# Rows 3 and 2 of the attention weights turned by VectorE and common transfers instead of by TensorE, with two rounds of buffers instead of three

## The chip, the cores and the metric

The kernel runs on one core of a Trainium2 chip. The metric is device time in microseconds; lower is better. Instructions run in order on each of five engines: TensorE (PE), VectorE (DVE), ScalarE (ACT), GpSimd (POOL) and SyncE (SP), which only starts transfers here. Engines wait for each other by semaphores.

## The reference

For x of 8 x 1024 tokens with 256 features the kernel computes `x + attention(layernorm(x)) + experts(layernorm(x))`, all in float32.

```python
qkv = jnp.einsum('bse,ehd->bshd', x, w_qkv)          # 16 heads of 64
logits = jnp.einsum('bqhd,bkhd->bhqk', q, k) / sqrt(64)
probs = softmax(where(causal_mask, logits, neg))
out = jnp.einsum('bshd,hde->bse', einsum('bhqk,bkhd->bqhd', probs, v), w_out)
```

The expert part routes each token to two of eight experts (256 to 1024 to 256, with relu), each with room for a limited number of tokens. The change touches the attention alone, which is also where the two parts are summed.

## The kernel before, in words

Layer norm, routing and the experts come first (about 900 us). Then `attention_and_sum` goes through 64 units, one for each batch and pair of heads. Precise products are made as three products of split operands (high and low parts), so each projection has a high copy by ScalarE and a low subtraction by VectorE.

A unit has the queries in eight rows of 128. Row i sees i + 1 blocks of 128 keys. The rows go in five rounds, `ROUNDS = [(3, 2), (4, 1), (5, 0), (6,), (7,)]`, each of four steps, so a unit has 20 steps. A round is a chain over the engines, for both heads h:

- TensorE: scores of the round into PSUM tile `S` (L1231). They wait until the minima of the round before are done, since `S` is used again.
- VectorE: row minima of the masked, negated scores, with a copy to SBUF, into a "room" `pr` (L1355).
- ScalarE: exponentials in place, with row sums (L1293).
- VectorE: reciprocals of the sums (L1361), at the start of the next round.
- GpSimd: scaling by the reciprocals, in place (L1436).
- Turning: the product with the values needs the weights with keys on the partitions.

There are two ways of turning. Rows 3, 2, 1 and 0 are transposed in 128x128 blocks by TensorE into a work bank in PSUM (L1187) and copied by ScalarE to `pT` (L1283). Rows 4 to 7 are transposed in squares of 32x32 by VectorE into `squares` (`square`, L1398), and transfers in strips of 32 partitions put them where they belong in `pT` (`place` on SyncE, L1085, and `place_rest` on GpSimd, L1465); there are 16 transfers for a group of two rows. Only after turning is a room free. `RING = 3` rounds of rooms take turns.

The product with the values (`values`, L1263) works on groups of two rows: one run for groups 0 and 1, one for group 2, one for group 3, each in the unit after. The result goes through ScalarE and VectorE (`oh`, `ol`) to the output projection (pieces o0 to o3, L1176), which VectorE adds to `res`.

Between the scores TensorE does pieces of other work in one of three PSUM banks: p0 to p3 (projections to q and k of the next unit, L1142), v0 and v1 (values of the pair after, L1157), xn (transposes of an input tile, L1165), t1 and t0 (rows 1 and 0 turned), o0 to o3. The order on all engines is written out by tables: `STEP_OF` says at which step TensorE does a piece, `ACT_STEP` and `DVE_STEP` at which step ScalarE and VectorE take it out of its bank, `BANK_OF` in which bank it lies, `RUN_STEP` when the values run, `POOL_AT` what GpSimd does when. Within a step VectorE does, in this order: reciprocals, the subtraction of a run, the pieces of the step, minima, and the squares of the round before in the third step of a round (`x == 2`). ScalarE does a run's copy, then pieces, then one exponential a step.

In the last unit all rows are turned by TensorE.

Of the kernel before, what the change touches and what calls it, by code (L numbers as in the profile page):

```python
# [16 lines left out]
P = 128  # L17
# [828 lines left out]
def attention_and_sum(nc, k, x, xn_dram, w_qkv, w_out, pick, y_dram, out, start):  # L846
# [10 lines left out]
    BL = 32  # L857
# [7 lines left out]
    SCALE_ORDER = [(i, h) for rows in ROUNDS for i in (rows if 0 not in rows else rows[::-1]) for h in range(2)]  # L865
# [10 lines left out]
    SQUARED = [4, 5, 6, 7]  # L876
    in_squares = lambda n, i: i in SQUARED and n < UNITS - 1


    TURNS = {"t30": [(3, 0, 0, 4)], "t31": [(3, 1, 0, 4)], "t20": [(2, 0, 0, 3)], "t21": [(2, 1, 0, 3)],  # L880
             "t1": [(1, 0, 0, 2), (1, 1, 0, 2)], "t0": [(0, 0, 0, 1), (0, 1, 0, 1)]}
    TURNS |= {f"t{i}{h}{c}": [(i, h, c * HT, min(HT, i + 1 - c * HT))] for i in SQUARED for c in range(-(-(i + 1) // HT)) for h in range(2)}


    STEP_OF = {"v0": 0, "xn": 1,
               "v1": 4, "o0": 5,
               "t30": 8, "t31": 8, "t20": 8, "t21": 8, "o1": 9, "p1": 10, "o2": 11,
               "p0": 12, "t1": 13,
               "t0": 16, "p2": 16, "p3": 17, "o3": 18}
# [17 lines left out]
    RUN_STEP = [(1, 3), (1, 7), (1, 15)]  # L907
# [11 lines left out]
    POOL_AT = {"split_w": 1, "total": 4, "place3": 5, "choose": 6, "fetch0": 8, "fetch1": 9, "weigh": 13, "add": 14, "place2": 16, "split_wv": 17}  # L919
# [24 lines left out]
    with ExitStack() as c:  # L944
# [45 lines left out]
        with ExitStack() as pre:  # L990
# [73 lines left out]
        def strip(g, a, b):  # L1064

            to, of = slice(b * BL, (b + 1) * BL), slice(a * BL, (a + 1) * BL)
            return wide[g][to, a].rearrange("p x r -> p (x r)"), sq[g][of, b].rearrange("p x k i -> p (x k i)")

        @block.sync
        def _(e):  # L1070
# [28 lines left out]
            for n in range(UNITS):  # L1099
# [18 lines left out]
                if n < UNITS - 1:  # L1118
                    place(n, 2)
# [12 lines left out]
        def _(e):  # L1132
# [103 lines left out]
            def values(n, j):  # L1236
                groups = RUN_GROUPS[j]
                if in_squares(n, 2 * groups[0]):
                    g = groups[0]
                    e.wait_ge(placed[g].sem, placed[g].at(n + 1, 0))  # L1240
                    e.wait_ge(pool_placed[g].sem, pool_placed[g].at(n + 1, 0))
                else:
                    for m, name in [(turn_unit(n, t), t) for g in groups for i in (2 * g, 2 * g + 1) for t in turns_of(i)]:
                        if by_act(name):
                            e.wait_ge(act.sem, act.at(m, name))
                        else:
                            e.wait_ge(dve.sem, dve.at(m, name))
# [91 lines left out]
        def _(e):  # L1339
            def row_min(n, j):  # L1340
# [69 lines left out]
            for n, s in ALL + END + [(UNITS + 1, s) for s in range(SUB)]:  # L1410
# [15 lines left out]
                if x == 2 and 0 <= m < UNITS and in_squares(m, ROUNDS[q][0]):  # L1426
                    for h in range(2):
                        square(m, ROUNDS[q][0], h)

        @block.gpsimd  # L1430
        def _(e):
# [28 lines left out]
            def place_rest(n, g):  # L1460
                e.wait_ge(squared.sem, squared.at(n, 4 * g - 4))
# [109 lines left out]
```

## Time and profile before

| | us |
|---|---|
| median of 3 runs | 2915.57 (2914.02 to 2918.3) |
| the profiled execution | 2915.7, its span 2913.9 |
| TensorE busy | 2814.5, 97% of the span |
| VectorE busy | 2084.7, 72% |
| GpSimd busy | 1723.0, 59% |
| ScalarE busy | 1699.7, 58% |
| mean granted clock of TensorE | 0.988 |

The shares are means over all stages. The attention part is the second half of the page's slices and more: there TensorE shows 9 tenths in every slice, VectorE 8, GpSimd 7 or 8, ScalarE 6. A matmul's row shows its start and modelled end; rows overlap, so from start to start is what one costs. The chain that ended last lies on TensorE for 66% of the span, by the page.

### The profile page before, as it was taken

How to read it: one execution, taken by the hardware profiler on the slowest of the kernel's cores; microseconds unless marked ns; L12 is line 12 of the kernel's file. 1: busy time of each engine (PE TensorE's matmuls, PEld its weight loads, DVE VectorE, ACT ScalarE, POOL GpSimd, SP SyncE). 2: the span in 40 equal slices, each digit the busy share in tenths (PEclk: the TensorE clock that was granted, in tenths of full speed). 3: DMA queues.
4: the chain of work that ended last, by engine and by line, in shares of the span. 5: the costliest groups of instructions: out<-in, count | busy, mean ns of one | idle time of the engine just before them, and what ended most of it. 6: DMA issues, size and time to landing. Idle time of an engine off the chain costs nothing.

```text
span 2913.9 us, 61264 instructions
## 1 busy us (share of the span) xinstructions
PE 2814.5 (97%) x21321; PEld 2284.1 (78%) x21321; DVE 2084.7 (72%) x4448; ACT 1699.7 (58%) x3934; POOL 1723.0 (59%) x2631
## 2 busy tenths in 40 slices
PE   5599999999998999999999999999999999999998
PEld 4489999899997777777777777777777777777776
DVE  7843444344434888888888888888888888888886
ACT  3454444445454666666666666666666666666664
POOL 3032122211212777777877877777777778777774
PEclk9799999999999999999999999999999999999999
DMA  7022212221212565665665565665665556556553
GB/s 241 29 82 75 69 52 83 76 68 47 82 54 74 141 158 144 163 154 145 168 150 145 147 170 147 157 166 142 157 164 151 149 146 176 141 145 183 136 134 93
DMA packets 248774, 371.58 MB, mean 128 GB/s; under 512 B 77392, under 2 KB 177744, under 8 KB 248480
## 3 DMA queue, kind: packets, MB, share of 16 engines
q1 hardware_dynamic: 216000, 276.31, 35.3%
q0 software_dynamic: 32480, 91.44, 11.7%
q8 instruction: 174, 2.85, 0.4%
q14 instruction: 120, 0.98, 0.1%
HBM read 102.80 MB, written 33.55 MB: 47 GB/s over the span
## 4 chain that ended last, share of the span: by engine, by line
PE 66%; DVE 1%; SPq 1%; DMA 0%; issue 0%; ACT 0%; POOL 0%; DVEq 0%; ACTq 0%
PE O L1263 18%; PE S L1231 16%; PE W L1142 12%; PE W L1157 7%; PE W L1176 7%; PE W L1187 6%; SPq L1085 1%; DVE pr L1355 0%; PE W L1165 0%; DMA pT<-squares 0%; DVE squares L1398 0%; ACT pr L1293 0%; DMA out<-res 0%; ACT pT L1283 0%; DVE res L1381 0%
## 5 line engine op out<-in xcount | busy, mean ns | idle before, releaser
L1436 POOL TENSOR_SCALAR pr<-pr,rinv 128x512 f32<-128x512 f32 (+7 forms) x1024 | 748.4, 744 | 399.7 <-DVE rinv L1361 398.6
L1293 ACT ACTIVATE pr<-pr,negm 128x512 f32<-128x512 f32 (+7 forms) x1024 | 787.3, 774 | 285.3 <-DVE negm L1355 285.3
L1355 DVE CUSTOM_DVE_ANT_0 pr<-S,late 128x512 f32<-128x512 f32 (+7 forms) x1024 | 717.0, 751 | 112.9 <-PE S L1231 112.9
L1263 PE MATMUL O<-pT,vv 128*64 128x256 f32 (+1 forms) x5120 | 541.3, 362 | 3.1 <-DMA pT<-squares 3.1
L1398 DVE STREAM_TRANSPOSE squares<-pr 128x640 f32<-128x640 f32 x504 | 494.8, 1020 | 0.0
L1263 PEld LDWEIGHTS O<-pT,vv 128*64 128x64 f32 x5120 | 346.4, 137 | 181.8 <-issue 20.4
L832 DVE TENSOR_TENSOR hl<-h,hh 128x512 fp32r<-128x512 f32 x256 | 192.3, 751 | 315.2 <-ACT hh L793 315.0
L789 ACT ACTIVATE h<-pH,b1c 128x512 f32<-128x512 f32 x256 | 175.9, 687 | 366.0 <-PE pH L719 334.1
L1283 ACT ACTIVATE pT<-W 128x512 f32<-128x512 f32 (+3 forms) x520 | 199.6, 437 | 215.8 <-PE W L1187 215.8
L731 PE MATMUL pY<-w2h,hh 128*128 128x256 f32 x1024 | 287.7, 281 | 2.5 <-DVE hl L832 2.5
L731 PE MATMUL pY<-w2l,hh 128*128 128x256 f32 x1024 | 289.1, 282 | 0.0
L731 PE MATMUL pY<-w2h,hl 128*128 128x256 f32 x1024 | 288.0, 281 | 0.0
L1465 POOL DMA_DIRECT2D pT<-squares x504 | 258.8, 521 | 0.3 <-issue 0.2
L1231 PE MATMUL S<-khf,qh 64*128 64x512 f32 (+2 forms) x1024 | 218.6, 422 | 3.6 <-DVE negm L1355 3.6
L1142 PE MATMUL W<-xnh,wh 128*128 128x512 f32 x512 | 215.1, 420 | 3.0 <-DVE klf L1389 1.5
L719 PE MATMUL pH<-xh,w1h 128*128 128x512 f32 x512 | 205.5, 401 | 4.2 <-DVE xl L804 2.6
L664 POOL COPY idx<-slot_token 128x4 uint32 (+1 forms) x30 | 8.8, 293 | 335.3 <-PE pX L705 335.3
L1142 PE MATMUL W<-xnl,wh 128*128 128x512 f32 x512 | 203.2, 397 | 0.0
L1142 PE MATMUL W<-xnh,wl 128*128 128x512 f32 x512 | 203.1, 397 | 0.0
L719 PE MATMUL pH<-xh,w1l 128*128 128x512 f32 x512 | 201.5, 394 | 0.0
L719 PE MATMUL pH<-xl,w1h 128*128 128x512 f32 x512 | 201.4, 393 | 0.0
L1381 DVE TENSOR_TENSOR res<-W,res 128x512 f32<-128x512 f32 x256 | 175.6, 686 | 35.6 <-PE W L1176 25.4
(176 smaller groups left out, 6479.6 us busy)
## 6 DMA issues: line engine op xcount, KB each, us to landing
pT<-squares SPq DMA_DIRECT2D x756, 128.0 KB
pT<-squares SPq DMA_DIRECT2D x756, 96.0 KB, 2.8
pT<-squares POOLq DMA_DIRECT2D x252, 128.0 KB
pT<-squares POOLq DMA_DIRECT2D x252, 96.0 KB, 3.0
y<-yb SPq DMA_DIRECT2D x128, 128.0 KB, 1.7
wr<-in_L_attn_w_qkv SPq DMA_DIRECT2D x128, 128.0 KB, 2.3
x<-in_L_attn_x SPq DMA_DIRECT2D x16, 512.0 KB, 8.9
xn<-xn SPq DMA_DIRECT2D x16, 512.0 KB, 4.4
```

What stands on the lines that cost most here:

```text
L719: ins = e.matmul(pH[hc % 4][:], w[par][:, m, ws], xx[q][:, m, :], start=(n == 0), stop=(n == 3 * MC - 1))
L731: ins = e.matmul(pY[t % 2][:], hs[q][:, hc, ts_], ws[par][:, hc, :], start=(hc == 0 and n == 0), stop=(hc == HC - 1 and n == 2))
L1142: ins = e.matmul(W, ws[:, 2 * m + of_k], xs[:, t0:t0 + HT, m, :], start=(i == 0), stop=(i == 3 * MC - 1))
L1157: ins = e.matmul(W[:, t * VW:(t + 1) * VW], xs[:, t0 + t, m, :], ws[:, m, :], start=(j == 0), stop=(j == len(terms) - 1))
L1176: ins = e.matmul(W[:, t * MODEL:(t + 1) * MODEL], os_[:, ts_], ws[:, of % PAIRS, :], start=(i == 0), stop=(i == 2))
L1231: ins = e.matmul(S[h][:, off + f * HALF:off + f * HALF + cols], t[hs, i * P:(i + 1) * P], u[f][n % 2][hs, 0:cols], start=(j == 0), stop=(j ...
L1263: ins = e.matmul(O[hs, o0 + a:o0 + GQ], vv[n // 2 % 2][:, kt, vs], turned_p, start=(kt == 0), stop=(kt == KT - 1))
L1293: e.activation(p, p, ACT.Exp, bias=negm[:, c0:c0 + 1], scale=-1.0, accum_out=rsum[:, c0:c0 + 1]).then_inc(expd.sem, 1)
L1355: e.tensor_tensor_reduce(room_of(n, i, h)[:, off:off + w], S[h][:, off:off + w], late[:, SEQ - w:], 1.0, -MASKED, ALU.add, ALU.min, negm[: ...
L1398: e.transpose(sq[g][:, :, 2 * h + i % 2, 0:KT, :], room_of(n, i, h)[:, OFFSET[i]:OFFSET[i] + KT * P].rearrange("p (k b i) -> p b k i", b=Q ...
L1436: e.tensor_scalar(p, p, rinv[:, c0:c0 + 1], 1.0, ALU.mult, ALU.mult).then_inc(scaled.sem, 1)
L1465: e.dma_start(*strip(g, QUARTERS - 1, b)).then_inc(pool_placed[g].sem, 16)
```

## The change

VectorE turns rows 3 and 2 (group 1) like rows 4 to 7: four more squares a unit, behind the minima of round 1. Groups 1 and 2 share tiles (`pT12`, `squares12`), so that one strip holds both: 16 transfers of 160 KB in place of 16 of 96 KB, all started by SyncE once row 5 is done; GpSimd starts 4 for group 3 alone. Fourteen transposes of TensorE and four copies of ScalarE go away. The larger squares take the space of a round of rooms: `RING` is 2. Row 1's transposes (t1) move from step 13 to 8, row 0's (t0) from 16 to 12, and both are scaled first in their rounds. The first run of values moves from step 3 to 7, and the tables are set anew. In the last unit only rows 6 and 7 are turned by TensorE.

```diff
-    SUB, RING = 4, 3
+    SUB, RING = 4, 2
-    SCALE_ORDER = [... (rows if 0 not in rows else rows[::-1]) ...]
+    SCALE_ORDER = [... (rows if 3 in rows else rows[::-1]) ...]
-    SQUARED = [4, 5, 6, 7]
-    in_squares = lambda n, i: i in SQUARED and n < UNITS - 1
+    SQUARED = [(i, h) for i in (3, 2, 4, 5, 6, 7) for h in range(2)]
+    in_squares = lambda n, i: i > 1 and (n < UNITS - 1 or i not in TURNED_LAST)
...
-    DVE_STEP = {"xn": 3, "o0": 6, "o1": 10, "p1": 12, "o2": 12, "p0": 15, "p2": 19, "p3": 19, "o3": STEPS + 2}
+    DVE_STEP = {"xn": 2, "p1": 6, "o0": 10, "o1": 10, "p0": 14, "o2": 15, "p2": 18, "p3": 19, "o3": STEPS}
...
-    RUN_STEP = [(1, 3), (1, 7), (1, 15)]
+    RUN_STEP = [(1, 7), (1, 11), (1, 15)]
...
+        pT12, sq12 = (sb(n, [P, QUARTERS, BLOCK[1] + BLOCK[2]]) for n in ("pT12", "squares12"))
...
             def place(n, g):
-                e.wait_ge(squared.sem, squared.at(n, 4 * g - 4))
+                e.wait_ge(squared.sem, squared.at(n, 4 * g))
...
-                for a in range(QUARTERS - 1):
+                for a in range(QUARTERS - (g == 3)):
...
             def square(n, i, h):
-                if n > 0 and i % 2 == 0 and h == 0:
-                    e.wait_ge(placed[g].sem, placed[g].at(n, 0))
-                    e.wait_ge(pool_placed[g].sem, pool_placed[g].at(n, 0))
+                if n > 0 and i in (3, 6) and h == 0:
+                    e.wait_ge(placed[max(g, 2)].sem, placed[max(g, 2)].at(n, 0))
...
-                if x == 2 and 0 <= m < UNITS and in_squares(m, ROUNDS[q][0]):
-                    for h in range(2):
-                        square(m, ROUNDS[q][0], h)
+                if x == 2 and 0 <= m < UNITS:
+                    for i in ROUNDS[q]:
+                        if in_squares(m, i):
+                            for h in range(2):
+                                square(m, i, h)
```

What the tables do to the order is seen in three places of a steady unit. On VectorE, between the minima of round 0 and of round 1 (`xnl` is piece xn, `squares 128x4x256` are row 7 of the unit before, `res` is an output piece, `ol` a run's subtraction), there stood before:

```order
L1381 TENSOR_TENSOR res<-W,res 128x512
L1398 STREAM_TRANSPOSE squares<-pr 128x4x256 x2
L1371 TENSOR_TENSOR xnl<-W,xnh 128x256
L1361 RECIPROCAL rinv<-rsum 128x4
L1405 TENSOR_TENSOR ol<-O,oh 128x512
L1355 ISA pr,negm<-S,late 128x640
```
and there stands now:

```order
L1379 TENSOR_TENSOR xnl<-W,xnh 128x256
L1407 STREAM_TRANSPOSE squares<-pr 128x4x256 x2
L1369 RECIPROCAL rinv<-rsum 128x4
L1363 ISA pr,negm<-S,late 128x640
L1363 ISA negm 128x1
```
The piece xn is ahead of the squares instead of behind them; the output piece and the run's subtraction are gone from here.

On VectorE, from the last minimum of round 1 to the first of round 2 (`klf` is piece p1), before:

```order
L1355 ISA pr,negm<-S,late 128x256
L1355 ISA negm 128x1
L1381 TENSOR_TENSOR res<-W,res 128x512
L1361 RECIPROCAL rinv<-rsum 128x4
L1405 TENSOR_TENSOR ol<-O,oh 128x256
L1355 ISA pr,negm<-S,late 128x768
```
and now:

```order
L1363 ISA pr,negm<-S,late 128x256
L1363 ISA negm 128x1
L1397 TENSOR_TENSOR klf<-W,khf 128x512
L1407 STREAM_TRANSPOSE squares<-pr 128x4x128 x2
L1407 STREAM_TRANSPOSE squares<-pr 128x4x96 x2
L1369 RECIPROCAL rinv<-rsum 128x4
L1414 TENSOR_TENSOR ol<-O,oh 128x512
L1363 ISA pr,negm<-S,late 128x768
```
Piece p1 and the four new squares stand ahead of the reciprocals of round 1.

On TensorE, behind the scores of round 2 (`W<-ident,pr` are transposes: fourteen of rows 3 and 2 before, four of row 1 now; `W<-woh,oh` and the like are an output piece), before:

```order
L1231 MATMUL S<-khf,ql 128x256 x2
L1187 MATMUL W<-ident,pr 128x128 x14
L1176 MATMUL W<-woh,oh 128x256
L1176 MATMUL W<-wol,oh 128x256
L1176 MATMUL W<-woh,ol 128x256
L1176 MATMUL W<-woh,oh 128x256
L1176 MATMUL W<-wol,oh 128x256
L1176 MATMUL W<-woh,ol 128x256
L1142 MATMUL W<-xnh,wh 128x512
```
and now:

```order
L1238 MATMUL S<-khf,ql 128x256 x2
L1194 MATMUL W<-ident,pr 128x128 x4
L1183 MATMUL W<-woh,oh 128x256
L1183 MATMUL W<-wol,oh 128x256
L1183 MATMUL W<-woh,ol 128x256
L1183 MATMUL W<-woh,oh 128x256
L1183 MATMUL W<-wol,oh 128x256
L1183 MATMUL W<-woh,ol 128x256
L1183 MATMUL W<-woh,oh 128x256
```
The transposes that stand here are now of a row of the round just ahead, and two output pieces follow them.

## Rows read from the trace of the kernel before

**Rows 1.** Window: length; busy PE, PEld, DVE, ACT, POOL; granted clock; DMA share; GB/s.
```profile
2000.00:2500.00 500.00, 500.00 (x4005) 388.52 (x4002) 419.81 (x930) 321.20 (x812) 388.14 (x617) 1.00 0.59 154
```

**Rows 2.** Timeline of VectorE, one unit: start, length (us), engine, line, operation.
```profile
2001.25 0.67 DVE L1355 CUSTOM_DVE_ANT_0 pr<-S,late 128x512 f32<-128x512 f32 x1
...
2003.41 0.69 DVE L1381 TENSOR_TENSOR res<-W,res 128x512 f32<-128x512 f32 x1
2004.01 2.36 DVE L1398 STREAM_TRANSPOSE squares<-pr 128x1024 f32<-128x1024 f32 x2
2006.30 0.38 DVE L1371 TENSOR_TENSOR xnl<-W,xnh 128x256 fp32r<-128x256 f32 x1
2006.61 0.16 DVE L1361 RECIPROCAL rinv<-rsum 128x4 f32<-128x4 f32 x1
...
2007.26 0.81 DVE L1355 CUSTOM_DVE_ANT_0 pr<-S,late 128x640 f32<-128x640 f32 x1
...
2009.43 0.69 DVE L1381 TENSOR_TENSOR res<-W,res 128x512 f32<-128x512 f32 x1
...
2016.44 1.56 DVE L1398 STREAM_TRANSPOSE squares<-pr 128x640 f32<-128x640 f32 x2
...
2018.63 0.69 DVE L1389 TENSOR_TENSOR klf<-W,khf 128x512 fp32r<-128x512 f32 x1 [0.31 <-ACT khf L1313]
...
2026.50 1.23 DVE L1355 CUSTOM_DVE_ANT_0 pr<-S,late 128x1024 f32<-128x1024 f32 x1 [0.87 <-PE S L1231]
...
2028.80 2.10 DVE L1398 STREAM_TRANSPOSE squares<-pr 128x896 f32<-128x896 f32 x2
...
2032.06 0.67 DVE L1355 CUSTOM_DVE_ANT_0 pr<-S,late 128x512 f32<-128x512 f32 x1
```

**Rows 3.** Timeline of TensorE, the same unit.
```profile
2008.85 2.60 PE L1263 MATMUL O<-pT,vv 128*64 128x256 f32 x24
2011.38 0.50 PE L1231 MATMUL S<-khf,qh 64*128 64x512 f32 x2
...
2012.98 1.89 PE L1187 MATMUL W<-ident,pr 128*128 128x128 f32 x14
...
2017.02 0.28 PE L1176 MATMUL W<-woh,oh 128*128 128x256 f32 x1
...
2017.83 0.50 PE L1231 MATMUL S<-khf,qh 64*128 64x512 f32 x2
...
2019.25 0.50 PE L1142 MATMUL W<-xnh,wh 128*128 128x512 f32 x1
...
2020.76 0.60 PE L1187 MATMUL W<-ident,pr 128*128 128x128 f32 x4
2021.29 3.46 PE L1263 MATMUL O<-pT,vv 128*64 128x256 f32 x32
...
2026.27 0.44 PE L1187 MATMUL W<-ident,pr 128*128 128x128 f32 x2
```

**Rows 4.** Timeline of ScalarE, the same unit.
```profile
2003.86 0.37 ACT L1299 ACTIVATE xnh<-W 128x256 fp32r<-128x256 f32 x1
...
2009.76 0.57 ACT L1304 ACTIVATE vv<-W 128x512 f32<-128x512 f32 x1
...
2017.99 0.60 ACT L1313 ACTIVATE khf<-W 128x512 fp32r<-128x512 f32 x1
...
2028.92 0.58 ACT L1313 ACTIVATE qh<-W 128x512 fp32r<-128x512 f32 x1
```

**Rows 5.** Timeline of GpSimd, the same unit.
```profile
2006.87 2.49 POOL L1436 TENSOR_SCALAR pr<-pr,rinv 128x512 f32<-128x512 f32 x4 [0.46 <-DVE rinv L1361]
```

**Rows 6.** Groups by form, scalings 256 wide: count, busy us, mean ns.
```profile
L1436 POOL TENSOR_SCALAR pr<-pr,rinv 128x256 f32<-128x256 f32 x32 | 14.8, 469 | 0.0
```

**Rows 7.** SyncE's transfers by line: ns of one issue, least, median, most.
```profile
L1085 SPq DMA_DIRECT2D pT<-squares x385: 507/592/1642, 1999.8 to 2492.9; - x193
```

**Rows 8.** Windows, ten microseconds near the start; columns as in rows 1.
```profile
30.00:40.00 10.00, 6.74 (x73) 5.38 (x66) 9.69 (x42) 4.30 (x14) 2.68 (x2) 0.73 1.04 366
```

More of the change, by code:

```diff
@@ L861, in attention_and_sum @@
     ROUNDS = [(3, 2), (4, 1), (5, 0), (6,), (7,)]
-    SUB, RING = 4, 3
+    SUB, RING = 4, 2
     STEPS = SUB * len(ROUNDS)
     ORDER = [(i, h) for rows in ROUNDS for i in rows for h in range(2)]
-    SCALE_ORDER = [(i, h) for rows in ROUNDS for i in (rows if 0 not in rows else rows[::-1]) for h in range(2)]
+    SCALE_ORDER = [(i, h) for rows in ROUNDS for i in (rows if 3 in rows else rows[::-1]) for h in range(2)]
     PLACE = {row: j for j, row in enumerate(ORDER)}
@@ new lines, in attention_and_sum @@
+    TURNS = {"t1": [(1, 0, 0, 2), (1, 1, 0, 2)], "t0": [(0, 0, 0, 1), (0, 1, 0, 1)]}
+    TURNS |= {f"t{i}{h}{c}": [(i, h, c * HT, min(HT, i + 1 - c * HT))] for i in TURNED_LAST for c in range(-(-(i + 1) // HT)) for h in range(2)}
+    STEP_OF = {"v0": 0, "xn": 1, "v1": 2,
+               "p1": 4,
+               "t1": 8, "o0": 9, "o1": 10,
+               "t0": 12, "p0": 12, "o2": 13,
+               "p2": 16, "p3": 17, "o3": 18}
+    ACT_STEP = {"v0": 2, "xn": 2, "v1": 4, "p1": 6, "t1": 8, "t0": 12, "p0": 13, "p2": 17, "p3": 18}
@@ L899, in attention_and_sum @@
+    DVE_STEP = {"xn": 2, "p1": 6, "o0": 10, "o1": 10, "p0": 14, "o2": 15, "p2": 18, "p3": 19, "o3": STEPS}
+    BANK_OF = {"v0": 0, "xn": 2, "v1": 1,
+               "p1": 2,
+               "t1": 2, "o0": 1, "o1": 0,
+               "t0": 2, "p0": 1, "o2": 0,
+               "p2": 0, "p3": 1, "o3": 2}
+    END_STEP = {6: (UNITS, 0), 7: (UNITS, 4)}
     DVE_STEP |= {f"t6{h}{c}": 2 for h in range(2) for c in range(2)}
@@ L953, in attention_and_sum @@
         vv = two(lambda i: sb(f"vv{i}", [P, QT, VW]))
-        pT = [sb(f"pT{g}", [P, 2, 2 * g + 2, GQ]) for g in range(GROUPS)]
-        sq = {g: sb(f"squares{g}", [P, QUARTERS, 4, 2 * g + 2, BL]) for g in (2, 3)}
-        wide = {g: pT[g][:].rearrange("p h k q -> p (h k q)").rearrange("p (a x r) -> p a x r", x=4, a=QUARTERS) for g in (2, 3)}
+        BLOCK = {g: 4 * (2 * g + 2) * BL for g in (1, 2, 3)}
+        pT0, pT3 = (sb(f"pT{g}", [P, 2, 2 * g + 2, GQ]) for g in (0, 3))
+        pT12, sq12 = (sb(n, [P, QUARTERS, BLOCK[1] + BLOCK[2]]) for n in ("pT12", "squares12"))
+        sq3 = sb("squares3", [P, QUARTERS, BLOCK[3]])
+        pT = {0: pT0[:], 3: pT3[:]}
+        wide = {1: pT12[:, :, :BLOCK[1]], 2: pT12[:, :, BLOCK[1]:],
+                3: pT3[:].rearrange("p h k q -> p (h k q)").rearrange("p (a r) -> p a r", a=QUARTERS)}
+        wide = {g: w.rearrange("p a (x r) -> p a x r", x=4) for g, w in wide.items()}
+        sq = {1: sq12[:, :, :BLOCK[1]], 2: sq12[:, :, BLOCK[1]:], 3: sq3[:]}
+        sq = {g: w.rearrange("p b (x k i) -> p b x k i", x=4, i=BL) for g, w in sq.items()}
+        whole = {2: (pT12[:], sq12[:]), 3: (wide[3].rearrange("p a x r -> p a (x r)"), sq3[:])}
         pr = start.pr + [sb(f"pr{i}", [P, SEQ]) for i in range(len(start.pr), 2 * RING)]
@@ L1026, in _ @@
             def _(e):
-                for g in (2, 3):
+                for g in (1, 2, 3):
                     e.memset(sq[g][:, :, 0::2, 2 * g + 1, :], 0.0)
@@ L1066, in strip @@
             to, of = slice(b * BL, (b + 1) * BL), slice(a * BL, (a + 1) * BL)
-            return wide[g][to, a].rearrange("p x r -> p (x r)"), sq[g][of, b].rearrange("p x k i -> p (x k i)")
+            placed_in, squares = whole[g]
+            return placed_in[to, a], squares[of, b]
         @block.sync
@@ L1117, in _ @@
                         refill(b, g)
-                if n < UNITS - 1:
-                    place(n, 2)
+                place(n, 2)
                 if n % 2 == 0 and n // 2 + 2 < UNITS // 2:
@@ L1237, in values @@
                 groups = RUN_GROUPS[j]
[L1238 to L1247, printed above, removed]
+                for g in groups:
+                    if in_squares(n, 2 * g):
+                        e.wait_ge(placed[max(g, 2)].sem, placed[max(g, 2)].at(n + 1, 0))
+                        if g == 3:
+                            e.wait_ge(pool_placed.sem, pool_placed.at(n + 1, 0))
+                    else:
+                        for m, name in [(turn_unit(n, t), t) for i in (2 * g, 2 * g + 1) for t in turns_of(i)]:
+                            if by_act(name):
+                                e.wait_ge(act.sem, act.at(m, name))
+                            else:
+                                e.wait_ge(dve.sem, dve.at(m, name))
                 if j == 0:
@@ L1518, in _ @@
                         place_rest(n - 1, 3)
-                    elif name == "place2" and n < UNITS - 1:
-                        place_rest(n, 2)
                     elif name == "choose":
```

33 lines of the change are left out of this document (10 added, 23 removed).

## The prediction

> **What bounds the kernel now.** I read the windows first, then one steady unit engine by engine. In 500 us of the attention part TensorE is busy for all 500.00 us, VectorE for 419.81, GpSimd for 388.14 and ScalarE for 321.20, and the granted clock is 1.00 [rows 1]. The reader should look for a gap in TensorE's list of a unit and find none: every row starts before the one ahead of it has ended [rows 3]. VectorE waits only where it needs scores, for 0.87 us before the minima of round 4 [rows 2]. So before the change TensorE sets the length of a unit: from the minima of round 0 to those of the next unit 2032.06 - 2001.25 = 30.81 us [rows 2], and there are 64 units.
>
> I write M0 to M4 for the moments at which VectorE starts the minima of rounds 0 to 4. In before M0 to M1 is 6.01 us and M4 to the next M0 is 5.56 [rows 2].
>
> **Part 1: fourteen transposes leave TensorE.** They take 1.89 us [rows 3]; nothing of rows 3 and 2 remains there. If TensorE stayed without gaps, a unit would take 30.81 - 1.89 = 28.92 us. The three copies of 512 columns and one of 384 that brought them from PSUM to SBUF leave ScalarE, which has slack [rows 1] and gains nothing I count.
>
> **Part 2: four transposes come to VectorE.** The trace has no pair 512 or 384 wide. A pair 1024 wide takes 2.36 us, one 640 wide 1.56 [rows 2]: 0.267 us for each 128 columns, which gives 1.29 and 1.03, less 0.07 each that the next instruction overlaps (2.36 long, but 2.29 from start to start): 2.18 us. Bounds: not above two pairs 640 wide, 3.12; not below what four copies of a plain 256-wide operation would cost at 0.31 (2006.30 to 2006.61 [rows 2]), 1.24. I take 2.18, since the shape of the instruction is the same and only the width differs. VectorE's work is then 419.81/500 x 30.81 + 2.18 = 25.87 + 2.18 = 28.05 us a unit, 97% of 28.92. Its waits decide.
>
> The Trainium skill, "VectorE: DVE Perf Modes", section Rules for kernel authors, speaks against the move: a full 128x128 transpose belongs on TensorE where PSUM will do as its target, and VectorE only turns 32x32 blocks. The rows agree mildly: TensorE pays 1.89/14 = 0.135 us a block, VectorE 2.18/14 = 0.156, and the blocks still need transfers. By the rule the trade loses 0.29 us of engine time a unit, by the trace it also moves the work to the engine that is about to be the fuller one.
>
> **Part 3: new places in VectorE's order make three waits.** In each, VectorE now takes a piece ahead of the squares that it took behind them, and the piece needs a ScalarE copy that stands behind two exponentials. (a) The subtraction of xn: the copy starts at 2003.86 and lasts 0.37 [rows 4], and 0.04 pass before VectorE can start (copy of khf 2017.99 + 0.60, subtraction 2018.63 [rows 4, 2]). So it starts at M0 + 3.02, while the minima end at M0 + 2.16 (2003.41): 0.86 of waiting. (b) p1: two exponentials of round 1 end at 2009.76, M1 + 2.50 [rows 4]; then the copy (0.60 + 0.04): M1 + 3.14 against minima that end at M1 + 2.17 (2009.43): 0.97. (c) p2: its copy starts at 2028.92 [rows 4], M4 + 2.42; with 0.58 and the same 0.04 VectorE can go on at M4 + 3.04, while the minima end at M4 + 2.30 (2028.80): 0.74. In before the squares (2.29 us after the minima of round 0, 2004.01 to 2006.30) covered exactly these copies. p0 gets such a wait too, but in round 3, where VectorE has room (below).
>
> **Part 4: row 1's four transposes now stand one round earlier.** In before, row 1 was turned on TensorE in round 3; now right behind the scores of round 2. Row 1 must first be scaled by GpSimd, that needs the reciprocals of round 1, and these stand on VectorE behind p1 and all four new squares. TensorE goes in order, so everything behind t1 waits: o0, o1, the values of group 2, the scores of round 3.
>
> **The sum, once round the unit.**
> M0 to M1: xn starts at 3.02, takes 0.31, squares of row 7 2.29, reciprocals 0.05 (0.65 from them to the next minima, with a 512-wide subtraction of 0.60 between, [rows 2]): 5.67.
> M1 to the reciprocals of round 1: 3.14, p1 0.60 (as 2003.41 to 2004.01), new squares 2.18: 5.92.
> Reciprocals to t1: 0.26 (2006.61 [rows 2] to 2006.87 [rows 5]), two scalings 256 wide at 0.47 [rows 6], 0.15 for GpSimd to TensorE (my choice between 0.04 above and the 0.23 from TensorE to VectorE, 2026.27 to 2026.50): 1.35.
> t1 to M3: t1 0.53 (2020.76 to 2021.29), two output projections at 0.81 (2017.02 to 2017.83), values of group 2 2.53 (2008.85 to 2011.38), scores of round 3 1.42 (2017.83 to 2019.25), 0.23: 6.33 [rows 3].
> M3 to M4 is TensorE's: 7.02 in before (2019.25 to 2026.27), without t1 0.53, with t0 0.27 and o2 0.81: 7.57.
> M4 to the next M0: 5.56 + 0.74 of (c) + o3, which now stands here, 0.60: 6.90.
> Together 33.74 us, against 30.81: +2.93.
>
> Is each leg the later of the two engines? TensorE reaches t1 early: scores of round 1 once the minima of round 0 are done (M0 + 2.16), 1.60, p1 1.51, values of groups 0 and 1 not over 2.53, scores of round 2 1.60 (2011.38 to 2012.98 [rows 3]): M0 + 9.40, while t1 can start at 5.67 + 5.92 + 1.35 = M0 + 12.94. It stands still for some 3.5 us. VectorE reaches the minima of round 3 early: 0.60 + 2.17 + 1.20 + 1.56 + 0.05 = 5.58 after the reciprocals, against 1.35 + 6.33. At M4 TensorE needs 1.51 + 1.51 + 0.81 + at most 1.60 = 5.43 to the end of the next scores, less than 6.90.
>
> **What I cost at nothing.** Two rounds of rooms instead of three: a room's squares already stand ahead of the minima that refill it, on the same engine. The common transfers: squares of row 5 are done by about M3 + 5.2; 16 issues at 0.592 [rows 7] take 9.5, so the last leaves at M3 + 14.7, and the squares of row 3 of the next unit, the first to need it landed, come at M3 + 7.57 + 6.90 + 5.67 + 3.74 = 23.9. That leaves 9 us for a landing; each further us would be one us a unit. The group read in strips by the values of group 1: hidden in TensorE's 3.5 us.
>
> 63 steps from unit to unit x 2.93 = 185 us. The profiled execution took 2915.7 us (span 2913.9, 1.8 around it), the median is 2915.57: the same. 2915.7 + 185 = 3100 us, my forecast. With the bounds of part 2 (-0.94 to +0.94 a unit) this case runs from 3041 to 3160.
>
> **Rivals.** (A) TensorE stays the bound: 28.92 a unit, 2915.7 - 63 x 1.89 = 2797 us. For it: TensorE had no gap at all. Against it: VectorE would have to be 97% busy with none of its three waits. (B) Only t1's wait is hidden, because VectorE runs ahead of my chain; then VectorE alone sets 28.05 + 0.86 + 0.97 + 0.74 = 30.62, -0.19 a unit: 2904 us, no change that could be told. Against it: the reciprocals stand behind the squares in the same queue, so nothing lets them run ahead. (C) Slower still: TensorE's clock falls after its new 3.5 us of standing. In 30 to 40 us of this trace TensorE was busy for 6.74 us of ten and the granted clock 0.73 [rows 8]: between full speed (2.4 GHz) and half of it, 54% of these ten us at half, which costs 2.7 us of work. Once a unit and wholly on the leg from t1 to M4 that is 33.74 + 2.7: 2915.7 + 63 x 5.63 = 3270 us; it decides from the point where the clock in a steady window drops below about 0.95. The Trainium skill, "TensorE: Matmul & The Clock Gate", section Why this matters for your kernels, warns of idle gaps between bursts for this reason; by it C would be the likeliest. The steady stretch shows 1.00 with no gap to test it on, and the new gap is a tenth of a unit where the slow stretch stood idle for a third.
>
> **Chances.** The forecast 0.68, C 0.14, B 0.10, A 0.08. Faster or slower means by over 0.2%, about 6 us; less than that cannot be told from no change here. Faster: A and half of B, 0.13; same: the other half, 0.05; slower: 0.82. The range leaves out A, B and the far end of C: 2990 to 3240; its low end is there for waits that overlap more than I let them.
>
> **What would show it.** Right: a unit near 33.7 us, TensorE's transposes of row 1 waiting some 3.5 us for GpSimd's scaling, VectorE waiting for ScalarE's copies at xn, p1 and p2, TensorE near 86% busy. Wrong: TensorE without a gap (A), a gap at t1 gone while VectorE is over 95% busy (B), a granted clock well below 1 (C), or VectorE's squares of row 3 waiting for transfers, which I priced at nothing.

## The result: slower by 7.4%, and the profile after

The changed kernel takes 3130.19 us (median of 4 runs, 3124.16 to 3133.84) where the kernel before takes 2914.8 on the same chip: a ratio of 1.0736, 95% interval 1.0713 to 1.0759. The forecast was 3100, the range 2990 to 3240. The profiled execution has a span of 3132.0 us, 218 more than before.

The page's busy times of the changed kernel, and then windows of it with the columns of [rows 1]: the same 500 us, one unit, and the unit ahead of it.

```profile
PE 2767.1 (88%) x20403; PEld 2237.2 (71%) x20403; DVE 2220.2 (71%) x4704; ACT 1589.3 (51%) x3674; POOL 1603.4 (51%) x2380
```

```profile
2000.00:2500.00 500.00, 439.24 (x3370) 338.15 (x3367) 403.42 (x876) 260.88 (x661) 314.77 (x485) 0.97 0.71 167
2017.82:2051.20 33.38, 29.27 (x232) 22.49 (x232) 27.83 (x62) 18.09 (x46) 23.14 (x37) 1.00 0.73 182
1982.94:2017.82 34.88, 30.74 (x232) 23.95 (x232) 28.00 (x62) 18.09 (x46) 20.96 (x33) 0.95 0.70 163
```

TensorE, without a gap in [rows 1], now stands for 12% of the time, and no other engine has become full: VectorE is busy for 403 of 500 us, less than before. So the time went into waits in a circle of engines, not into work. Two lengths of a unit stand side by side: 33.38 us at a granted clock of 1.00, and 34.88 at 0.95.

VectorE in the unit at clock 1.00, against [rows 2]: start, length, engine, line, operation, and in brackets the idle time before it and who ended it.

```profile
2017.82 0.67 DVE L1363 CUSTOM_DVE_ANT_0 pr<-S,late 128x512 f32<-128x512 f32 x1
...
2020.85 0.42 DVE L1379 TENSOR_TENSOR xnl<-W,xnh 128x256 fp32r<-128x256 f32 x1 [0.78 <-ACT xnh L1307]
2021.19 2.36 DVE L1407 STREAM_TRANSPOSE squares<-pr 128x1024 f32<-128x1024 f32 x2
...
2023.53 0.79 DVE L1363 CUSTOM_DVE_ANT_0 pr<-S,late 128x640 f32<-128x640 f32 x1
...
2026.62 0.69 DVE L1397 TENSOR_TENSOR klf<-W,khf 128x512 fp32r<-128x512 f32 x1 [0.85 <-ACT khf L1321]
2027.22 2.21 DVE L1407 STREAM_TRANSPOSE squares<-pr 128x512 f32<-128x512 f32 x4
2029.36 0.13 DVE L1369 RECIPROCAL rinv<-rsum 128x4 f32<-128x4 f32 x1
...
2036.87 1.09 DVE L1363 CUSTOM_DVE_ANT_0 pr<-S,late 128x896 f32<-128x896 f32 x1 [0.71 <-PE S L1238]
...
2044.32 1.23 DVE L1363 CUSTOM_DVE_ANT_0 pr<-S,late 128x1024 f32<-128x1024 f32 x1 [0.87 <-PE S L1238]
...
2047.35 0.69 DVE L1397 TENSOR_TENSOR ql<-W,qh 128x512 fp32r<-128x512 f32 x1 [0.65 <-ACT qh L1321]
...
2051.20 0.68 DVE L1363 CUSTOM_DVE_ANT_0 pr<-S,late 128x512 f32<-128x512 f32 x1
```

TensorE and GpSimd of the same unit, against [rows 3] and [rows 5]; of TensorE, the last piece ahead of its long wait is p1.

```profile
2020.22 0.50 PE L1238 MATMUL S<-khf,qh 64*128 64x512 f32 x2 [0.42 <-DVE negm L1363]
...
2022.53 0.47 PE L1149 MATMUL W<-xnh,wh 128*128 128x512 f32 x1 [0.64 <-ACT vv L1312]
...
2030.69 0.63 PE L1194 MATMUL W<-ident,pr 128*128 128x128 f32 x4 [2.60 <-POOL pr L1447]
```

```profile
2020.95 1.44 POOL L1459 TENSOR_TENSOR wl<-wr,wh 128x256 fp32r<-128x256 f32 x2
...
2026.17 0.73 POOL L1511 TENSOR_TENSOR res<-res,yg 128x256 f32<-128x256 f32 x1
2026.84 2.09 POOL L1476 DMA_DIRECT2D pT<-squares  x4
...
2029.60 2.50 POOL L1447 TENSOR_SCALAR pr<-pr,rinv 128x256 f32<-128x256 f32 x4 [0.47 <-DVE rinv L1369]
```

The reader should follow one hand-over: reciprocals of round 1 on VectorE at 2029.36, behind the four new squares; GpSimd's scaling of row 1 at 2029.60; TensorE's t1 at 2030.69, after 2.60 us of standing.

The length of all 63 intervals between the minima of round 0, before and after, accounts for the difference:

| intervals | before, us each | after, us each | difference, us |
|---|---|---|---|
| 47 plain ones, as if all at 33.40 | 30.81 | 33.40 | 121.6 |
| 28 of these, longer at the lower clock | | 34.86 | 40.8 |
| 7 in which a batch's output is stored | 30.6 to 32.7 | 35.5 to 39.1 | 39.0 |
| 7 plain ones at the end, without xn | 30.57 | 32.21 | 11.4 |
| the first two | 24.90, 34.02 | 30.94, 34.00 | 6.0 |

Together 218.8. The first and fourth lines are the chain of the forecast, the second is a falling clock. The third holds the chain too, and beyond it waits for transfers behind SyncE's queue and a clock of 0.95 or less in all seven; these two aren't separated here. The first two units are not traced back.

The clock, in windows of two microseconds of the longer unit:

```profile
1992.00:1994.00 2.00, 1.23 (x18) 0.93 (x14) 2.00 (x4) 1.17 (x5) 2.00 (x5) 1.00 0.86 213
1994.00:1996.00 2.00, 0.18 (x1) 0.21 (x2) 2.00 (x7) 0.00 (x0) 1.53 (x5) 0.92 0.98 281
1996.00:1998.00 2.00, 2.00 (x11) 2.00 (x11) 1.38 (x8) 1.06 (x3) 1.85 (x3) 0.50 1.05 250
1998.00:2000.00 2.00, 2.00 (x14) 1.65 (x15) 1.29 (x2) 2.00 (x7) 1.43 (x2) 0.72 1.02 227
2000.00:2002.00 2.00, 2.00 (x22) 1.32 (x20) 1.63 (x4) 0.25 (x3) 0.27 (x1) 1.00 0.31 84
```

TensorE stood 2.59 us ahead of t1, which starts at 1995.82. At about the end of that stand the granted clock fell to 0.50, the lower level of 1.2 GHz, and it was back at 2.4 in the window from 2000. The output projection's matmuls start 0.21 us apart at the lower level, and 0.12 in the other unit.

SyncE and then TensorE where a batch ends (the interval from 2051.20 is 36.5 us long):

```profile
2044.88 0.37 SPq L1102 DMA_DIRECT2D res<-in_L_attn_x  x1
2045.34 11.85 SPq L1093 DMA_DIRECT2D pT<-squares  x16
2057.24 1.74 SPq L1085 DMA_DIRECT2D wvr<-in_L_attn_w_qkv  x2
2059.02 0.51 SPq L1097 DMA_DIRECT2D out<-res  x1
2062.28 0.37 SPq L1102 DMA_DIRECT2D res<-in_L_attn_x  x1
```

```profile
2061.04 3.80 PE L1271 MATMUL O<-pT,vv 128*64 128x256 f32 x24 [3.47 <-issue]
```

The sixteen common transfers leave only behind the third quarter's store and refill, up to 2057.19. The first run of values of the next unit reads them and starts at 2061.04, after 3.47 us for which the row names no releaser. The last of the sixteen was issued at 2056.4 and took 4.4 us to land, so it landed at 2060.8, just ahead of the run; I read the wait as one for this landing, and experiment 6 tests it.

### The profile page after: what moved, and what is told of

Read it like the earlier page. It is cut to its first block and busy times, and to the rows that moved or that the text cites. A ratio compares the mean times of both kernels' runs of the same rounds, so it can differ in the third digit from the quotient of the medians.

```text
span 3132.0 us, 58788 instructions
## 1 busy us (share of the span) xinstructions
PE 2767.1 (88%) x20403; PEld 2237.2 (71%) x20403; DVE 2220.2 (71%) x4704; ACT 1589.3 (51%) x3674; POOL 1603.4 (51%) x2380
## 5 line engine op out<-in xcount | busy, mean ns | idle before, releaser
L1407 DVE STREAM_TRANSPOSE squares<-pr 128x512 f32<-128x512 f32 x764 | 639.4, 882 | 1.2 <-DMA pT<-squares 1.2
L1271 PE MATMUL O<-pT,vv 128*64 128x256 f32 (+1 forms) x5120 | 556.3, 369 | 31.9 <-issue 11.9
L1271 PEld LDWEIGHTS O<-pT,vv 128*64 128x64 f32 x5120 | 356.7, 140 | 227.6 <-issue 46.6
L1149 PE MATMUL W<-xnh,wh 128*128 128x512 f32 x512 | 219.7, 429 | 42.0 <-ACT vv L1312 34.4
L1291 ACT ACTIVATE pT<-W 128x256 f32<-128x256 f32 (+1 forms) x260 | 73.0, 332 | 304.7 <-PE W L1194 298.8
L1332 ACT ACTIVATE oh<-O 128x256 fp32r<-128x256 f32 (+1 forms) x192 | 86.5, 451 | 250.9 <-PE O L1271 250.7
L1194 PE MATMUL W<-ident,pr 128*128 128x128 f32 x414 | 85.3, 327 | 143.3 <-POOL pr L1447 139.8
L731 PEld LDWEIGHTS pY<-w2h,hh 128*128 128x128 f32 x1024 | 193.0, 188 | 7.9 <-issue 2.9
```

The source lines that it names most:

```text
L731: ins = e.matmul(pY[t % 2][:], hs[q][:, hc, ts_], ws[par][:, hc, :], start=(hc == 0 and n == 0), stop=(hc == HC - 1 and n == 2))
L1149: ins = e.matmul(W, ws[:, 2 * m + of_k], xs[:, t0:t0 + HT, m, :], start=(i == 0), stop=(i == 3 * MC - 1))
L1271: ins = e.matmul(O[hs, o0 + a:o0 + GQ], vv[n // 2 % 2][:, kt, vs], turned_p, start=(kt == 0), stop=(kt == KT - 1))
L1332: e.activation(oh[:, cols], O[:, cols], ACT.Copy).then_inc(ohi.sem, 1)
L1407: e.transpose(sq[g][:, :, 2 * h + i % 2, 0:KT, :], room_of(n, i, h)[:, OFFSET[i]:OFFSET[i] + KT * P].rearrange("p (k b i) -> p b k i", b=Q ...
```

## The experiments

Times are medians; the kernel before stood between 2914 and 2918 us beside them. BEH, NOPOOL and ORD name edits that later kernels use again.

**1. Filling TensorE's gap.** Nine matmuls of 512 columns, whose result nothing reads, ahead of t1.

```diff
+ if n < UNITS and s == 8:
+     e.wait_ge(act.sem, act.at(n if n + 1 < UNITS else n - 1, "v0"))
+     for j in range(9):
+         e.matmul(banks[0], wh[:, 0], xnh[:, 0:HT, 0, :], start=True, stop=True)
```

> The changed kernel with nine extra matmuls of 512 columns (some 2.1 us, their result is thrown away) on TensorE between the scores of round 2 and row 1's transposes, where it stands idle for 2.6 us. Theory (chain, and the clock falls because of that idle stretch): row 1's transposes start when they did, the chain is as long as before (33.4 us a unit), but no unit is seen at a granted clock of 0.95 any more, which 36 of 63 are in the changed kernel at 1.5 us each: about 3076 us, mean clock near 0.99. Rival 1 (the clock has another cause, the alternation of units is one of even and odd pairs): still 34.9 every other unit, about 3130. Rival 2 (TensorE is the bound after all): 63 x 2.1 us more, 3260.

3108.5 us, ratio 1.0656 (1.0636 to 1.0676). Windows of a unit, then the filler in it:

```profile
1967.61:2001.01 33.40, 31.59 (x241) 24.11 (x241) 27.84 (x62) 18.09 (x46) 20.97 (x33) 1.00 0.73 170
```

```profile
1977.82 2.37 PE L1283 MATMUL W<-xnh,wh 128*128 128x512 f32 x9
1980.49 0.63 PE L1194 MATMUL W<-ident,pr 128*128 128x128 f32 x4 [0.30 <-POOL pr L1451]
```

All plain units are 33.40 at clock 1.00: the standing time brought the clock down there, and the chain does not care whether TensorE works or waits. The clock still falls in four of the seven batch ends. These grew (36 to 39.5 us), and the last units to 32.9, so the total fell by 22 us and not by the 54 expected.

**2. The three pieces behind the squares again (BEH).**

```diff
- DVE_STEP = {"xn": 2, "p1": 6, ... "p2": 18,
+ DVE_STEP = {"xn": 3, "p1": 7, ... "p2": 19,
```

> The changed kernel with the pieces xn, p1 and p2 taken by VectorE behind the squares instead of ahead of them (DVE_STEP 3, 7 and 19 instead of 2, 6 and 18). Theory: the three waits for ScalarE's copies (0.78, 0.85 and 0.65 us in the changed kernel, 2.3 to 2.6 us with what hangs on them) leave the closed chain: 33.4 - 2.5 = 30.9 us a unit; TensorE's wait at row 1's transposes shrinks from 2.6 to about 0.6 us and the clock stays up: about 2930 us in all. Rival 1 (VectorE's own load and the transposes in it set the length): the load is the same, so the time moves by less than 0.5 us a unit, over 3080 us. Rival 2 (common transfers late): no change either.

2992.73 us, 1.0276 (1.0249 to 1.0303): the largest step of any experiment, 137 us. By the traces the shorter chain of the 47 plain units gives 100 us and the clock, which no longer falls in them, 41; the rest moved a little the other way. The plain unit falls by 2.13, to 31.27, though TensorE still waits:

```profile
1918.75 0.63 PE L1194 MATMUL W<-ident,pr 128*128 128x128 f32 x4 [0.98 <-POOL pr L1447]
```

In that unit the three legs with the moved pieces are shorter by 0.87, 0.96 and 0.73 us, 2.56 together as expected. The leg from the reciprocals to M3 gave 0.43 back (7.94 for 7.51): GpSimd starts the scaling 0.69 us after the reciprocals and not 0.24. The time missed the 2930 expected by 63 us, mostly at the batch ends, which are 36.6 to 38.9 us.

**3. t1 behind the output projections.**

```diff
- "t1": 8, "o0": 9, "o1": 10,
+ "o0": 9, "o1": 10, "t1": 11,
```
(and ScalarE's copy of it at step 12.)

> The changed kernel with row 1's transposes on TensorE moved from step 8 to 11, behind two output pieces (o0, o1). Theory: the pieces wait only for the subtraction of the first run, which VectorE does 0.6 us after the reciprocals of round 1, so TensorE goes on 0.8 us after them instead of 1.3: 0.5 us a unit less at the same clock (32.9), about 3095 us if the clock falls as often as now, down to 3045 if it stays up. Rival 1 (GpSimd's scaling of row 1 alone is what holds TensorE): taking it off the path wins far more, 2 us a unit or more, under 3000 us. Rival 2 (not this place holds the unit): no change.

3127.96 us, 1.0717 (1.0691 to 1.0743). The unit at clock 1.00 is 32.98, as expected, but 38 of the 47 plain units are 34.5 at 0.95, where 28 were at 0.95 in the changed kernel. The circle runs through o0 as well: it needs the first run's subtraction, which stands behind the same squares.

```profile
2029.81 0.53 PE L1183 MATMUL W<-woh,oh 128*128 128x256 f32 x1 [2.13 <-DVE ol L1414]
```

**4. The new squares one block wide.** Rows 3 and 2 are turned for 128 columns only; the rest of their transposing is left out.

```diff
+ KT = 1 if i < 4 else KT
```

> The changed kernel with VectorE's four squares of rows 3 and 2 cut to one block of 128 columns each (32 columns a strip), which leaves that part of the transposing out; transfers, waits and order are as before. Theory: the four squares take about 0.6 us instead of 2.15 and the reciprocals behind them come 1.5 us earlier: 31.9 us a unit and, with 1.1 us of idle time left at row 1's transposes, a clock that stays up: about 2985 us. Rival 1 (a chain that does not hold these squares sets the length): no more than 0.5 us a unit, over 3080 us.

3119.72 us, 1.0695 (1.0676 to 1.0715); 32.87 at clock 1.00, where 31.9 was expected, and 36 of the 47 plain units are some 34.4 at 0.95, where the clock was to stay up. The squares took 0.88 us, not 2.21, but GpSimd wasn't ready:

```profile
1954.84 0.88 DVE L1408 STREAM_TRANSPOSE squares<-pr 128x128 f32<-128x128 f32 x4
1955.64 0.14 DVE L1369 RECIPROCAL rinv<-rsum 128x4 f32<-128x4 f32 x1
```

```profile
1953.78 0.73 POOL L1512 TENSOR_TENSOR res<-res,yg 128x256 f32<-128x256 f32 x1
1954.45 2.08 POOL L1477 DMA_DIRECT2D pT<-squares  x4
1956.53 0.20 POOL L1482 COPY sel<-pick 128x4 uint32<-128x4 uint32 x1
1956.70 2.48 POOL L1448 TENSOR_SCALAR pr<-pr,rinv 128x256 f32<-128x256 f32 x4
```

The reciprocals came at 1955.64, the scaling 1.06 us later, behind four DMA issues. In the changed kernel GpSimd idled only 0.47 us there: whoever takes more than half a microsecond from the squares meets its queue. By the length of the unit alone, shorter by 0.53 us, the rival is nearly met (no more than 0.5); GpSimd's rows are why I read it otherwise, and the next experiment tests that.

**5. GpSimd issues none of the third group (BEH and NOPOOL).**

```diff
- for a in range(QUARTERS - (g == 3)):
+ for a in range(QUARTERS):
```
(and `place_rest` goes, with its semaphore.)

> e2_behind with the four transfers of group 3 that GpSimd starts (2.08 us of its time) started by SyncE with the other twelve. Theory (GpSimd's queue, full until half a microsecond after the reciprocals of round 1, is what held row 1's transposes in e4_small and e2_behind): TensorE's wait there shrinks from 0.98 to about 0.4 us, a steady unit from 31.27 to about 30.7 us, some 35 us in all, 2955 us; the units at a batch's end stay at 37 to 39 us or grow, since SyncE has four more transfers ahead of the common ones. Rival (VectorE's squares alone hold it): no change, 2990 us.

3003.0 us, 1.0306 (1.0285 to 1.0327), no better than experiment 2. The best units are 30.85, near the 30.7 expected, with TensorE's wait at t1 down from 0.98 to 0.56 us, so GpSimd's queue did hold it in part. But units scatter up to 32.4 and batch ends reach 37 to 40.5: SyncE now issues 32 strips a unit, and TensorE waits for the third group's.

**6. The common transfers ahead of the third quarter's store (BEH and this).**

```diff
-                    for g in range(3):
+                    for g in range(2):
                         store(b - 1, g)
-                    for g in range(3):
+                    for g in range(2):
                         refill(b, g)
                 place(n, 2)
+                if b > 0 and u == 0:
+                    store(b - 1, 2)
+                    refill(b, 2)
```

> e2_behind with SyncE's order changed in the first unit of a batch: the common transfers of groups 1 and 2 ahead of the store and refill of the third quarter of the output, instead of behind them. Theory: the seven units of 36.6 to 38.9 us against 31.3 are units in which the common transfers leave late, because SyncE waits for that store to land; with the new order they come down to 31 to 32.5 us, 40 us less in all: about 2950 us, steady units unchanged. Rival (the store's and refill's traffic slows them): no change, 2990 us.

3006.39 us, 1.0312 (1.0291 to 1.0334). It failed: batch ends are 40.0 to 40.8 us. The first run's wait is gone, but SyncE now stands for two landings of stores ahead of the third group, and another run of values waits:

```profile
1985.52 0.67 SPq L1097 DMA_DIRECT2D out<-res  x1
1990.13 0.37 SPq L1102 DMA_DIRECT2D res<-in_L_attn_x  x1
...
1992.13 18.21 SPq L1093 DMA_DIRECT2D pT<-squares  x27
```

```profile
2001.86 5.87 PE L1274 MATMUL O<-pT,vv 128*64 128x256 f32 x32 [6.30 <-DMA pT<-squares]
```

**7. All of these together.** BEH, NOPOOL, the order of experiment 6, t1 at step 11, p1 in another PSUM bank, p0 behind its squares too, and GpSimd's weight split one unit ahead.

```diff
-               "p1": 2,
-               "t1": 2, "o0": 1, "o1": 0,
+               "p1": 0,
+               "o0": 1, "o1": 0, "t1": 2,
...
-    POOL_AT = {"split_w": 1, ...
+    POOL_AT = {"split_w": 18, ...
```

> All together: pieces behind the squares (p0 too), all transfers by SyncE, the store order of e6_store, row 1's transposes behind o0 and o1, piece p1 in a bank that does not wait for xn, and GpSimd's split of the next weights at step 18 of the unit before instead of step 1. Theory: the waits of TensorE in e2_behind (0.18, 0.88 and 0.98 us a unit) go but for 0.3 us, so a unit is TensorE's 28.9 plus 0.3 to 0.8 us, and the whole takes 2810 to 2845 us, faster than both kernels. Rival (VectorE, 28.05 us of work and waits of its own of over 2 us, sets the length): over 30.1 us a unit, 2890 us or more.

2966.93 us, 1.0178 (1.0159 to 1.0198). The plain units are 30.44 to 31.15, 18 of 47 at 30.45 or less and most below the 30.81 of before, but none at the 29.2 to 29.7 expected. Six of the batch ends are 38.8 to 42.4. One long wait was left on TensorE in a unit:

```profile
1874.07 0.35 PE L1185 MATMUL W<-woh,oh 128*128 128x256 f32 x1 [1.02 <-DVE ol L1412]
```

**8. Fewer waits for a landing in SyncE's way (BEH and ORD).** Transfers go ahead of the later stores, and the refills of the last two quarters one unit later; the refills of the first two still wait for their stores.

```diff
                 if b > 0 and u == 0:
-                    for g in range(3):
+                    for g in range(2):
                         store(b - 1, g)
-                    for g in range(3):
+                    for g in range(2):
+                        refill(b, g)
+                if b > 0 and u == 1:
+                    for g in (2, 3):
                         refill(b, g)
                 place(n, 2)
+                if b > 0 and u == 0:
+                    store(b - 1, 2)
...
                     store(b - 1, 3)
-                    refill(b, 3)
```

> As e2_behind, with SyncE's order changed in the two units in which a batch ends: each common transfer is issued ahead of the store that waits for the later output projections, and the refills of the third and fourth quarter of the residual go one unit later, behind the third group's transfers, when their stores have long landed; nothing is left out. Theory (the long units at the ends of batches come from transfers that stand in SyncE's queue behind waits for stores): the 7 long units of e2_behind (36.6 to 38.9 us) come to 31.3 to 32 us, the others stay at 31.27, so 2993 - 7 x 6.2 = about 2950 us. Rival (the long units come from the bytes that stores, refills and strips move at the same time): they stay at 36 us or more and the time within 10 us of 2993.

2973.86 us, 1.0191 (1.0174 to 1.0208): 19 us better than experiment 2, where 43 were expected. The batch ends were 36.6 to 38.9 us and are now 33.5 to 37.1; what the seven take beyond plain units fell from 46 to 31 us together, by the traces, so the order of the queue was a third of it. In the unit from 1967.66, with the DMA engines at 0.95, TensorE still waited for the third group's strips:

```profile
1991.89 4.97 PE L1275 MATMUL O<-pT,vv 128*64 128x256 f32 x32 [4.24 <-DMA pT<-squares]
```

**9. ORD in the kernel of experiment 7, and p1 behind the first run's subtraction.**

```diff
- DVE_STEP = {"xn": 3, "p1": 7, ...
+ DVE_STEP = {"xn": 3, "p1": 8, ...
```

> As e7_all with the order of SyncE's queue of e8_order in place of its own, and with the subtraction of the key projection behind that of the first run of values on VectorE; nothing is left out. Theory: the boundary units of e7_all (38.8 to 42.4 us) fall to 30.5 to 31.5 (-62 us in all), and TensorE's wait of 1.02 us ahead of the first output projection falls to about 0.4, which takes a unit from 30.45 to about 29.9 (-30 us): 2967 - 62 - 30 = about 2875 us, under the kernel before. Rival (the unit is bound elsewhere on VectorE by then, and the order of two subtractions doesn't matter): units stay at 30.4 and the time is about 2905 us, no gain over the kernel before worth the name.

2910.54 us, 0.9981 (0.9970 to 0.9991): level with the kernel before. Batch ends 32.6 to 34.4, plain units 30.37 and not 29.9. The wait ahead of o0 fell from 1.02 to 0.64 only:

```profile
2030.12 0.36 PE L1186 MATMUL W<-woh,oh 128*128 128x256 f32 x1 [0.64 <-DVE ol L1413]
```

**10. GpSimd issues the refills.**

```diff
- POOL_AT = { ... "total": 4, ...
+ POOL_AT = { ... "total": 4, "fill2": 6, "fill3": 9, "fill0": 17, "fill1": 17, ...
```

> As e9_all, with all refills of the residual issued by GpSimd in place of SyncE; nothing is left out. In e9_all's unit 33 (33.01 us beside 30.37 for the others) SyncE issues without a pause from 1900 to 1958 us, each half of 16 strips in about 11.5 us, and TensorE waits 2.46 us for the third group's strips. Theory (SyncE's queue is too full in that pair of units: waits for stores and refills take 6 us of it): the 7 boundary units fall from 32.6 to 34.2 to 30.4 to 31, and the time by about 16 us, to 2895. Rival (the DMA engines, busy 0.93 of that unit, are full, and whoever issues doesn't matter): the units stay at 32.6 or more, the time at 2910.

2930.01 us, 1.0038 (1.0025 to 1.0051). My theory fell, and the time is above the rival's 2910 too: batch ends rose to 34.7 to 36.6, and TensorE's wait for the third group there is 3.99 us (2.46 in experiment 9).

```profile
1964.41 5.15 PE L1258 MATMUL O<-pT,vv 128*64 128x256 f32 x32 [3.99 <-DMA pT<-squares]
```

Refills landed 6.2 us after their issue instead of 3.7. The Trainium skill, "Trainium Kernel Development and Optimization", section Key Constraints, says that queues of several engines share the same 16 DMA engines, and that issuing from more of them saves only issue time; this run agrees in that nothing was gained (2930 us and not 2910). How much of a batch end is full DMA engines, and how much the later refills, these runs don't separate.

**11. The squares of row 2 behind the first run's subtraction, and ScalarE's copy of p1 later.**

```diff
+ if n < UNITS and s == 2 * SUB:
+     for h in range(2): square(n, 2, h)
- if in_squares(m, i):
+ if in_squares(m, i) and i != 2:
```

> As e9_all, with the squares of row 2 (two of the four of 128x512) behind the first run's subtraction on VectorE, ahead of the row minima whose rooms they free, and ScalarE's copy of p1 behind that run's copy; nothing is left out. In e9_all the first output projection waits 0.64 us for that subtraction, which starts when the fourth square ends. Theory (the row of squares ahead of the subtraction is what TensorE still waits for): the subtraction starts 0.5 us earlier, TensorE's wait falls to about 0.1, a unit from 30.37 to about 29.85, the time from 2910 to about 2883 us. Rival (TensorE then waits for the scaled rows or VectorE for the same scores, and the chain keeps its length): units of 30.2 or more, 2900 us or more.

2927.73 us, 1.0040 (1.0028 to 1.0052), units of 30.83, longer than the 30.37 of experiment 9. o0's wait fell to 0.17 as expected, and another took its place:

```profile
2011.51 0.36 PE L1186 MATMUL W<-woh,oh 128*128 128x256 f32 x1 [0.17 <-DVE ol L1413]
...
2018.76 0.41 PE L1197 MATMUL W<-ident,pr 128*128 128x128 f32 x2 [1.18 <-POOL pr L1449]
```

**12. t0 behind p0 and o2 as well.**

```diff
- "t0": 12, "p0": 12, "o2": 13,
+ "p0": 12, "o2": 13, "t0": 14,
```
(and ScalarE's copy of t0 at step 16 and not 12.)

> As e11_split, with row 0's transposition on TensorE (t0) behind the query projection and the third output projection, and ScalarE's copy of it three steps later; nothing is left out. In e11_split the wait ahead of the first output projection fell from 0.64 to 0.17 us as expected, but TensorE then waited 1.18 us for GpSimd's scaled row 0 at t0, and the unit grew to 30.83. Theory (that wait took the place of the one removed, and nothing else stands close behind): t0's wait goes, the unit falls by about 1.1 to 29.7, VectorE's waits shrink alike, and the time falls to about 2860 us, below the kernel before. Rival (VectorE, 27.5 us busy in a unit, and its handovers with TensorE's scores hold the chain at its length, so another wait appears): units of 30.4 or more, 2900 us or more.

2896.74 us, 0.9922 (0.9908 to 0.9935), faster than the kernel before by 0.8%. The expected 2860 was not reached, but t0's wait is gone; a unit's windows:

```profile
2018.79:2048.49 29.70, 29.27 (x235) 22.84 (x234) 27.49 (x62) 17.86 (x46) 21.02 (x33) 1.00 0.79 183
```

TensorE is busy for 29.27 of 29.70 us: in such a unit it is the bound, as rival A described, if not at A's 28.92. They are 22 of the 47 plain units (29.63 to 29.74 us). All others but one are 29.9 to 31.3, the next one (30.89) with a wait of TensorE of 1.16 us for the third group's transfers, and batch ends are 33 to 35.4.

## Why the prediction was right, and where it was off

**The chain.** Its legs, predicted and measured in the unit from 2017.82: M0 to M1 5.67 and 5.71; M1 to the reciprocals 5.92 and 5.83; to t1 1.35 and 1.33; t1 to M3 6.33 and 6.18; M3 to M4 7.57 and 7.45; M4 to M0 6.90 and 6.88; the sum 33.74 and 33.38. That TensorE left the lead to this circle was the decisive step, and experiment 2 shows it from the other side: moving three subtractions back gave 2.13 us a unit.

One reading of the kernel before was wrong: VectorE does not wait only for scores there. Ahead of the reciprocals of round 1 it stands for ScalarE's exponentials:

```profile
2011.35 0.18 DVE L1361 RECIPROCAL rinv<-rsum 128x4 f32<-128x4 f32 x1 [1.23 <-ACT pr L1293]
```

The new squares stand where this wait was. So the leg from M1 to these reciprocals grew by 1.74 us (4.09 to 5.83), less than the squares' own 2.14, although a new wait of 0.85 stands in it too. The sum was not touched, since it added the leg up anew.

**The three waits** were 0.78, 0.85 and 0.65, predicted 0.86, 0.97 and 0.74. **The new squares** took 2.14 us from start to start, predicted 2.18. The Trainium skill ("VectorE: DVE Perf Modes", section Rules for kernel authors) would leave 128x128 transposes to TensorE where PSUM will do as the target; going against it cost 0.25 us of engine time a unit by the trace (2.14 against 1.89 [rows 3]). The order of three subtractions around the squares cost 2.13 (experiment 2).

**TensorE's standing** was put at 3.5 us and is 2.60. It reached t1 0.87 later than I reckoned (M0 + 10.27, not 9.40): scores started 0.24 later, and p1 waited 0.64. The row names ScalarE for that, but GpSimd's `wl` ended at 2022.39, 0.14 us ahead of p1: a hand-over I hadn't priced, harmless here because the slack was there. TensorE is busy for 88%, predicted 86.

**Rival C was half true.** The forecast had no term for the clock, and a chance of 0.14 for it. 28 of 47 plain units lost 1.46 us to it, 41 us in all; I had priced it at 2.7 in each unit. Experiment 1 shows the cause for the plain units.

**"What I cost at nothing".** Two rounds of rooms cost nothing: the minima of round 2 follow the first run's subtraction at once, and the squares of row 3 start without a wait. The common transfers cost nothing in a plain unit, though sixteen issues took 11.85 us and not 9.5. At a batch's end they do cost: I worked them out in a unit without stores, and the stores' waits stood ahead of them in SyncE's queue. The 7 batch ends gained 39 us, some 17 of it by the chain and 22 beyond it; in the kernel of experiment 2, another order of the queue took away a third of what they cost beyond plain units (experiment 8). How much of the 22 is the clock, at 0.95 or less in all seven, stays open.

So the sum missed two things, the clock in plain units (+41) and the batch ends (+22). It overrated two: the chain by 0.34 in a plain unit (-18, over 53 of them), and the last eight, where a unit without xn grew by 1.63 and not 2.93 (-10). 185 + 41 + 22 - 18 - 10 is 220, against 218.8 measured. The mechanism is the one the forecast named: the chain gave some 150 of the 219 us (121.6, 17 and 11.4). That the time came out within 30 us is in part luck: 63 us, over a quarter of the slowdown, had no term in the sum, and 28 that it overrated hid nearly half of them.

**The other rivals.** A, TensorE alone, and B, VectorE alone, were wrong for this kernel. A was right on what limits the unit once the order is mended: it took all the edits up to experiment 12 to get there, and then in 22 of 47 units.

## What to carry to other kernels

Work taken from the engine that never waits pays only if what it then waits for is ready earlier by as much: price a change of order as a circle of hand-overs (here reciprocals, scaling, t1, scores), leg by leg, and look at what each queue holds ahead of the piece that moves. When a wait goes, look for the next one within half a microsecond of it; here experiments 2, 4, 7, 9 and 11 each met another, and only experiment 12 has units in which TensorE runs through. Check transfers that share a queue in the unit where other work stands in it too, not only in the plain one.

## What the runs showed of the hardware

The granted clock fell after 2.59 us of standing in one unit and not after 2.60 in the next; why they differ stays open. Where it fell, a plain unit grew by 1.46. In experiments 3 and 4 TensorE's longest stand in most plain units is some 2.1 us, and the clock fell in 38 and 36 of the 47; in experiment 2, with 1.0 us (1.5 in one unit), it fell in none.

The run of sixteen strips by SyncE above took 0.74 us a strip on average. Its median issue, 0.602 us, is hardly longer than the 0.592 before [rows 7]; a few issues take up to 1.31, so a median times sixteen is too little for a run. GpSimd's four took 2.09 us, 0.52 each.
